# Earlier first loads, reordered tails and a bias add moved to GpSimd in a fused four-layer kernel

## What is computed

```python
x = L0_attn_x                                              # (2, 1024, 512)
# 1. time mix: k, v, r = x@Wk.T, x@Wv.T, x@Wr.T; w = exp(clip(k)), first token times exp(time_first)
#    num = decay*num + w*v ; den = decay*den + w over the tokens ; out = (sigmoid(r) * num/(den+1e-6)) @ Wo.T
x = _layernorm(x + _L0_attn_ref(...))
# 2. feed forward with Walsh-Hadamard transforms: h = fwht(x*SU_ug)/64
#    silu(h@W_gate.T * s_g) * (h@W_up.T * s_u), fwht(. * SU_dp)/64, @W_down.T * s
x = _layernorm(x + _L0_ffn_ref(...))
# 3. causal attention, 16 heads of 32, sin/cos positions: softmax(q k^T / sqrt(32)) v @ out_w.T + out_b
x = _layernorm(x + _L1_attn_ref(...))
# 4. shared expert plus the 2 best of 8 routed experts (bf16), weighted by the router's softmax
x = _layernorm(x + _L1_ffn_ref(...))
```

## Time and profile before

| what | value |
| --- | --- |
| median of 3 runs | 1600.88 us (1598.05 to 1601.29) |
| profiled execution: its own time / span / mean granted clock | 1599.74 us / 1598.0 us / 0.975 |
| PE busy | 1489.6 us (93%), 7696 matmuls |
| DVE / ACT / POOL busy | 990.5 (62%) / 613.4 (38%) / 459.8 us (29%) |
| DMA | 223.40 MB, mean 140 GB/s |
| time mix and its tail | 0 to 229.6 us |
| feed forward | to about 790 |
| q/k/v | to 938 |
| attention | to 1281 |
| projection, experts | to 1598 |

### The profile page before, as it was taken

One profiled execution on the slowest core, in us unless ns is written; L12 is line 12 of the kernel. 1 busy time (PEld: TensorE's weight loads), 2 busy tenths in 40 slices (PEclk: granted clock), 3 DMA queues, 4 the chain that ended last, 5 costly groups with the idle time before them and its releaser, 6 DMA issues. The chain is left out here.

```text
span 1598.0 us, 22563 instructions
## 1 busy us (share of the span) xinstructions
PE 1489.6 (93%) x7696; PEld 1084.6 (68%) x7696; DVE 990.5 (62%) x1916; ACT 613.4 (38%) x1079; POOL 459.8 (29%) x385
## 2 busy tenths in 40 slices
PE   6999889999999999999998989999999898897996
PEld 4787768788888888888876764444444376674554
DVE  4977967854545554552432757777777375466664
ACT  4343444623422431341211025554555634231554
POOL 0433343302421440340432122221222224003760
PEclk9999989999999999999999989999999998998998
DMA  5111536503321430424257573666662566712336
GB/s 184 44 62 53 189 112 226 195 27 130 94 66 40 145 104 0 132 79 160 110 184 232 172 201 106 177 177 190 191 187 100 201 255 226 289 56 70 102 98 224
DMA packets 105182, 223.40 MB, mean 140 GB/s; under 512 B 9281, under 2 KB 35265, under 8 KB 104193
## 3 DMA queue, kind: packets, MB, share of 16 engines
q1 hardware_dynamic: 101344, 211.96, 40.9%
q0 software_dynamic: 3744, 10.23, 2.1%
HBM read 157.54 MB, written 64.36 MB: 139 GB/s over the span
## 5 line engine op out<-in xcount | busy, mean ns | idle before, releaser
L1861 ACT ACTIVATE at_pt<-at_st 128x512 f32<-128x512 f32 (+3 forms) x384 | 164.2, 497 | 140.4 <-PE at_st L1893 139.6
L898 POOL TENSOR_TENSOR ff_w_lo<-ff_raw,ff_w_hi 128x1024 fp32r<-128x1024 f32 x64 | 153.8, 2405 | 210.8 <-ACT ff_w_hi L928 210.8
L115 PE MATMUL op_bank<-ff_x_hi,ff_w_lo 128*128 128x512 f32 x512 | 200.2, 391 | 0.0
L117 PE MATMUL op_bank<-ff_x_hi,ff_w_hi 128*128 128x512 f32 x512 | 200.0, 391 | 0.0
L116 PE MATMUL op_bank<-ff_x_lo,ff_w_hi 128*128 128x512 f32 x512 | 199.9, 391 | 0.0
L1159 DVE TENSOR_TENSOR ff_h_lo<-ff_hf,ff_h_hi 128x512 f32 (+1 forms) x64 | 149.6, 2337 | 53.6 <-ACT ff_h_hi L1047 53.3
L1893 PE MATMUL at_st<-mx_qp,mx_kp 98*128 98x512 f32 (+3 forms) x288 | 104.4, 395 | 15.9 <-ACT at_pt L1861 10.6
L928 ACT ACTIVATE ff_w_hi<-ff_raw 128x1024 fp32r<-128x1024 f32 x64 | 67.8, 1061 | 118.3 <-PE op_bank L117 116.0
L115 PEld LDWEIGHTS op_bank<-ff_x_hi,ff_w_lo 128*128 128x128 f32 x512 | 96.7, 189 | 20.3
L116 PEld LDWEIGHTS op_bank<-ff_x_lo,ff_w_hi 128*128 128x128 f32 x512 | 96.7, 189 | 20.2
L117 PEld LDWEIGHTS op_bank<-ff_x_hi,ff_w_hi 128*128 128x128 f32 x512 | 96.6, 189 | 20.4
(11 more groups left out here) (450 smaller groups left out, 3352.8 us busy)
## 6 DMA issues: line engine op xcount, KB each, us to landing
ff_raw<-in_Wug SPq DMA_DIRECT2D x64, 512.0 KB, 3.6
at_raw<-in_expert_gu SPq DMA_DIRECT2D x16, 704.0 KB, 12.2
mx_qp<-q_hi SPq DMA_DIRECT2D x12, 512.0 KB, 5.6
mx_kp<-k_hi SPq DMA_DIRECT2D x12, 512.0 KB, 11.3
at_raw<-in_expert_d SPq DMA_DIRECT2D x8, 768.0 KB, 14.2
expert_gu_bf<-at_cast SPq DMA_DIRECT2D x16, 352.0 KB, 10.9
ex_e_gu<-expert_gu_bf SPq DMA_DIRECT2D x8, 704.0 KB, 8.4
tm_raw_x<-in_xT SPq DMA_DIRECT2D x4, 1024.0 KB, 6.4
```

The lines of the kernel that those rows point to most:

```text
L115: pe.matmul(out, cut_l(ll), cut_r(rh), start=first, stop=False, **kw)
L117: return pe.matmul(out, cut_l(lh), cut_r(rh), start=False, stop=last, **kw)
L898: pool.tensor_tensor(w[j][1][:, :, :, :], raw[:, j], f32(w[j][0][:, :, :, :]), ALU.subtract)\
L1861: act.activation(pt[:, s % PT, h, off:TB], st[(s * HG + h) % ST][:, off:TB], ACT.Exp, scale=SCALE).then_inc(exp_done, 1)
```

## The change

1. **First loads.** Block 0 of x^T and Wk are loaded in four quarters of 256 KB each, alternately. ACT and DVE split quarter by quarter (`first_high`, `first_low`), and PE starts a channel tile k when its quarter is split. All four weights have a raw buffer of their own, so Wv, Wr, Wo are issued at once. PE's order in block 0 is k0, k1, v0, v1, r0, r1 and then tiles 2 and 3 as before.
2. **Time mix, DVE.** `add(i-1)` stands before `x_low(i+1)`.
3. **Tail.** ACT's `prepare` and the first two `sign` stand before `high(3, 2)`. DVE's `x_low` is made in two pairs between tiles 1, 2 and 3 of `add(2)`. `fold.build` and `cross_low(0)` stand before `add(3)` on DVE, `fold.signs` and `cross_high(0)` before the scales of blocks 2 and 3 on ACT.
4. **q/k/v.** `turn(i+1)` moves from n = 1 to n = 3, `x_high` from 4 to 5, `x_low` from 5 to 6. The loads of unit 0 go two per n at n = 0 to 3. The wait for the stores of v moves from the end of q/k/v to SP's list in attention.
5. **Projection, experts.** A class `Kept` gives the residual four homes, two of them over the last 16 KB of `pt`, so no load waits for a store. The bias is added on POOL, one 128x2048 operation per block. `project(3)` moves into the expert stage, with two pairs of `turn(0, k)` behind its tiles 1 and 2, and PE waits for all added tiles only before its second product group. DVE's `add(3)` is cut in three around the two pairs of `x_low(0)`. ACT's `x_high(0)` goes ahead of `scale(2)`. `sd_lo` goes behind the first `x_bf`, and root(2) ahead of `su_lo`.

The core of the diff:

```diff
-        load_x(0)
-        load_w(0)
+        for k in range(KT):
+            sp.dma_start(raw_x[:, k, :], x_dram[:, k, 0:TB]).then_inc(first_loaded[k], DMA)
+            sp.dma_start(raw_w[0][:, k, :], w_dram[0][:, k, :]).then_inc(first_loaded[k], DMA)
         load_w(1)
+        load_w(2)
+        load_w(3)
...
+        def first_high():
+            for k in range(KT):
+                act.wait_ge(first_loaded[k], 2 * DMA)
+                act.activation(x_hi[:, 0, k, :], raw_x[:, k, :], ACT.Copy).then_inc(first_hi, 1)
+                act.activation(w[0][0][:, k, :], raw_w[0][:, k, :], ACT.Copy).then_inc(first_hi, 1)
...
+                    if s == 0 and n == 0:
+                        pe.wait_ge(first_hi, 2 * k + 2)
+                        pe.wait_ge(first_lo, 2 * k + 2)
...
-        for m in range(KT):
+        for n in range(PROJ):
+            project(0, 0, [n])
+            project(0, 1, [n])
+        for m in range(2, KT):
             project(0, m)
...
+            if norm:
+                add(i - 1)
             if more:
                 x_low(i + 1)
-            if norm:
-                add(i - 1)
...
-            high(i, 2)
             if tail:
                 ff.prepare(act)
                 ff.sign(act, 0, 0)
                 ff.sign(act, 0, 1)
+            high(i, 2)
...
-                if i >= NB - 2 and n < mx.LOADS:
-                    mx.load_part(sp, i - (NB - 2), n)
+                if i == NB - 2:
+                    for part in range(2 * n, min(2 * n + 2, mx.LOADS)):
+                        mx.load_part(sp, 0, part)
+                if i == NB - 1 and n < mx.LOADS:
+                    mx.load_part(sp, 1, n)
...
-                if n == 1 and i < NB - 1 :
+                if n == KT - 1 and i < NB - 1:
                     turn(pe, i + 1)
...
+    def add_bias(self, pool, i):
+        if i == 0:
+            pool.wait_ge(self.ow.bias_loaded, DMA)
+        self.ln.wait_loaded(pool, i)
+        rows = self.ln.block(i)
+        pool.tensor_tensor(rows, rows, self.ow.bias[:, :].rearrange("p (o c) -> p o c", o=1).to_broadcast([P, TT, C]), ALU.add)\
+            .then_inc(self.biased, 1)
...
+            for stored in mx.v_stored:
+                sp.wait_ge(stored, NB * TT // 2 * DMA)
             ow.load(sp, a)
...
+            if c == 1:
+                pe.wait_ge(out.ln.added, NT)
...
-        pe.wait_ge(small_loaded, DMA)
-        for k in range(KT):
-            turn(0, k)
+        def turn_first(t):
+            if t == 0:
+                pe.wait_ge(small_loaded, DMA)
+            elif t < TT - 1:
+                turn(0, 2 * t - 2)
+                turn(0, 2 * t - 1)
+
         pe.wait_ge(freed, UNITS * 2 * 2)
-        pe.wait_ge(out.ln.added, NT)
+        out.project(pe, NB - 1, turn_first)
...
-        x_low(0)
+        out.add(dve, NB - 1, (0, 1))
+        x_low(0, (0, 1))
+        out.add(dve, NB - 1, (2,))
+        x_low(0, (2, 3))
+        out.add(dve, NB - 1, (3,))
```

173 lines of the change are left out of this document (107 added, 66 removed).

## The result

The changed kernel takes 1584.03 us (1583.71 to 1585.33, 4 runs) against 1601.09 (1598.05 to 1604.95, 4 runs) for the kernel before: ratio 0.9894, interval 0.9872 to 0.9916. That is 17 us less. The forecast was 1573.3, 28 us less. The profiled execution has a span of 1582.1 us against 1598.0, 15.9 less.

The account below looks back on a forecast made before the run. PE's waits, 45.6 us together, were taken as the bound. Time mix and tail 9.0, q/k/v 10.5 and projection and experts 8.0 sum to 27.5 off 1599.74, 1572.2, or 1573.3 as the median; range 1562 to 1587.

Parts of the forecast that it names:

- the last DMA's own lead: Experts: the DMA staging block 1 goes out at 1334.8 instead of 1342.36, limiting the gain to about 8.0 us.
- Step 1, the start: Block 0 of time mix: PE starts near 6.5 us instead of 13.2, lead 8.6, or 7.0 if the clock drops.
- Step 2, blocks 1 and 2: Time mix: `add` ahead of `x_low` shrinks waits of 2.5 and 1.7 us to 0.9 and 0; lead grows to 11.3.
- Step 3, the tail: End of time mix: early sign gains 0.6, later silu lengthens the crossing wait; net -2.5 us, bounds -4 and +1.5.
- Step 4, q/k/v: Later turn 5.0, earlier loads of unit 0 3.6, barrier without v's stores 1.9: sum 10.5 us, bounds 6 and 13.
- I count 3.6 of the 4.4: q/k/v: loading unit 0 two per step issues the seventh load some 16 us earlier, saving 3.6 of a 4.4 us wait.
- the second rival: q/k/v: doubled loads hold up the stores, PE waits for a part, 3.6 + 1.4 us lost, time 1578.3; chance 0.09.
- my own signs of being wrong: DVE's first wait near zero with PE idle in blocks 0 to 2, L1756 above 9 us, or PE's part wait in q/k/v.
- Step 5, projection and experts: PE restarts about 10.8 us sooner at the experts, but the staged block 1 limits the gain to 8.0, bounds 3 and 11.
- It now goes out at about 1334.8, after the first `x_bf`, and lands near 1342.2: Experts: the DMA staging block 1, before issued at 1342.36 and landed at 1349.75; PE wants it at 1339.8 and waits 2.4.
- The rival of the lock: Projection: POOL's bias, 19.2 us, can stop DVE's lows for as long; 9.2 us later, time 1581.3; chance 0.10.
- The rival on the slower side: Projection and experts: POOL's bias operations above 9.1 us each delay the experts; 1596.8 at 13.0, 1604.8 at 15; chance 0.03.

Follow-up runs that it names:

- part 5 alone: Kernel before with only the projection and experts changes (bias on GpSimd, four residual homes, project(3) with the turns inside): 1598.7 us, ratio 0.9983.

## Why the prediction was right or wrong

The direction and the range held, the size was 1.6 times too large: 27.5 us forecast, 17 measured (15.9 between the profiled executions). The bounds of the terms, added up, reach from 1566 to 1589 and not, as written, from 1563 to 1582; the measured 1584.03 lies inside the first and outside the second. The range of the forecast held because it left room for several small losses at once, and that is what came. Two more slips are small: the part on the start adds 15.8 and 10.9 to 26.9, and the last DMA's own lead is 7.5 by its rows and not 8.0.

- **Step 1, the start.** Right to 1 us. PE began at 7.5 and not near 6.5, and Wv landed at 12.5 instead of 11.5, behind eight smaller DMAs. The lead was 7.6, between my 8.6 and 7.0. The prediction's estimate from the page "DMA: Bandwidth & Descriptors" of the Trainium skill (section Bandwidth) was a loss of 0.8 us; Wv's 1.0 agrees with it in size. But the trace does not show slower transfers as the reason: the last two pairs of quarters landed 1.33 and 1.37 us apart, as fast as the 1.4 us per 512 KB of before, and the delay is in the first two (5.37 and 7.08 where I had 4.6 and 6.0). Of the lead 1.6 us are luck of the trace: in the kernel with part 5 alone, whose start is that of the kernel before, PE waits 1.44 us for Wr's low and not 2.42, the clock stays at its full level behind it, and PE is 1.6 us ahead.
- **Step 2, blocks 1 and 2.** Right: 11.3 forecast, 10.65 measured, waits of 1.10 and 0 where I had 0.9 and 0. What I did not see is that without this step the start would have kept only 5.1.
- **Step 3, the tail.** The amount was right (-2.5 forecast, -2.0 in the feed forward), and that was luck: two errors cancel. I charged the loss to the later statistics, root(2) and `w_low`, and credited the early sign with +0.6. The wait for `ff_w_lo` did come (2.86 us), but it took the place of the 2.1 us wait, and the undone sign gives the 2 us back by itself. The sentence "The wait moves, longer, so I count a gain of 0.6 only" lacked both the length (5.89 us for 3.48) and the clock.
- **Step 4, q/k/v: 10.5 forecast, 5.6 measured.** The failed term is "I count 3.6 of the 4.4" for the loads of unit 0. The wait for `mx_vv` went away entirely, but 4.5 us of waits for `qkv_whole` came instead, with the lower clock behind each. With single loads q/k/v gives 6.5 us, with the doubled ones 5.6. So the term is not +3.6 but nought or a little less, and the turn and the barrier, 6.9 forecast, are what gave the 6.5 (the barrier's wait 1.9, as forecast). This is the second rival, priced at 5.0 lost, and 4.9 is what the step lost. It had a chance of 0.09 and was simply true, and a wait of PE in q/k/v's block 2 was among my own signs of being wrong. The rows were there: in the kernel before, ACT's `part_hi` already waited 2.7 us for a store beside single loads.
- **Attention and feed forward, "keep their lengths".** The feed forward did, to 0.1 us. Attention lost 0.7 us net: the lower clock came at other moments in it. That is less than traces of the same code differ by.
- **Step 5, projection and experts: 8.0 forecast, 2.0 measured.** PE's lead at its first products was 7.8 to 10.0, where I had 8.5 to 10.8. The failed term is "It now goes out at about 1334.8, after the first `x_bf`, and lands near 1342.2". With the lead of 13.6 us taken out, it went out at 1338.8 and landed at 1346.0, 4 us later than I had it. The 7.2 us of the DMA itself were right. What was missing is what stands ahead of `x_bf(0)` on POOL: root(3), which waits for `scale(2)`, which ACT now does after `x_high(0)`. A wait of 2.1 us for ACT's `ex_logits_t`, behind ACT's `scale(3)` and a table load, was new too. It takes PE's lead over the kernel before, the 13.6 included, from 23.6 to 21.4 us, and the staged block with what follows to 15.5.
- **GpSimd's bias.** 4.8 us per block forecast, 4.6 measured. The rival of the lock was right in its mechanism (6 of the 10 us are paid back) and wrong in its price for the time. By the rule on the shared port in "SBUF — State Buffer" of the Trainium skill (section "SBUF: two separate sides") the one that comes second is blocked for the whole of the other's instruction. The DVE row of 3.46 us, which ends 0.55 us after POOL's bias and takes 0.69 us without it, agrees. The rival on the slower side, a bias above 9 us, was far off.

## What to carry to other kernels

When a DMA on the path is made earlier, ask what else is in the queue at that moment and who waits for its landing: here doubled loads held up small stores, and those held up the buffers of the next step; spreading the same loads over more time, from an earlier start, gave in the trace what bunching them did not. A wait that is moved behind more work can end up longer than the two it replaces, and can cost the clock on top, so a reorder has to be measured by the lead at a matmul further down. And an operation that releases the next stage's load belongs at the front of its engine's list, with its stores kept out of the way.
